# A decoder layer on one core: attention rounds in another order, routing steps with one tensor input, and 110 expert tiles

## The reference

```
x = layernorm(x + mamba(x))                    # state space scan
x = layernorm(x + xattn(x, ctx))               # cross attention, 16 heads of 16 channels, RoPE
x = layernorm(x + ffn(x))                      # mixture of experts and a shared expert

xattn: Q = rope(x)Wq + bq, K = rope(ctx)Wk + bk, V = ctx Wv + bv
       out = softmax(Q K^T / 4) V, then Wo, bo
ffn:   logits = x gate_w^T                     # 15 experts
       the 3 largest are chosen; weights = softmax, renormalised over the 3
       y  = sum over the 3 of weight * ((gelu(x W_g) * (x W_u) * mult) fc2 + b)
       ys = the same with the shared expert's weights, for every token
       out = y + ys
```

## Time and profile before

| | us |
|---|---|
| median of 3 runs | 2185.69 (2179.36 to 2189.15) |
| the profiled execution | 2181.16 |
| its span | 2179.3 |
| busy: PE / DVE / ACT / POOL | 1697.8 / 1588.5 / 1042.0 / 1248.0 |
| granted TensorE clock, mean | 0.906 of full speed |

### The profile page before, as it was taken

How to read it: one execution, slowest core, us unless ns; L and a number is a source line. 1 busy time by engine, 2 the same in 40 slices (tenths; PEclk the granted TensorE clock), 3 DMA queues, 4 the chain that set the end, 5 groups by cost and what they waited for, 6 DMA issues and landing times. The chain is left out here.

```text
span 2179.3 us, 32460 instructions
## 1 busy us (share of the span) xinstructions
PE 1697.8 (78%) x9684; PEld 1089.3 (50%) x9685; DVE 1588.5 (73%) x2792; ACT 1042.0 (48%) x2354; POOL 1248.0 (57%) x840
## 2 busy tenths in 40 slices
PE   5688778778777778534787888777498999999695
PEld 4344444444444444213455555555385555555484
DVE  3699999999899999965478888875223555555278
ACT  3677777777777777620233333333112333333221
POOL 0889888898889899847547776633200222222100
PEclk9899998999899999657799999988699999999897
DMA  5544444555554455414833333331541222222332
GB/s 162 116 115 114 113 111 108 116 117 117 117 117 116 103 123 114 111 60 97 211 106 109 123 105 113 110 106 38 177 163 36 79 82 82 80 81 82 139 128 77
DMA packets 178820, 238.24 MB, mean 109 GB/s; under 512 B 24001, under 2 KB 114113, under 8 KB 176642
## 3 DMA queue, kind: packets, MB, share of 16 engines
q1 hardware_dynamic: 161426, 201.73, 35.4%
q0 software_dynamic: 9984, 28.06, 3.6%
q10 hardware_dynamic: 7280, 6.83, 1.2%
HBM read 169.70 MB, written 66.84 MB: 109 GB/s over the span
## 5 line engine op out<-in xcount | busy, mean ns | idle before, releaser
L268 POOL TENSOR_TENSOR inject<-dx_n,bc_n 128x2048 f32<-128x2048 f32 x128 | 578.9, 4533 | 147.5 <-DMA dx_n<-dup_rows 84.7
L401 ACT ACTIVATE ps_h<-delta_n,a_neg 128x256 f32<-128x256 f32 x1024 | 424.9, 462 | 110.9 <-DVE hc L537 73.5
L524 DVE TENSOR_TENSOR_SCAN ps_h<-ps_h,inject 128x1024 f32<-128x1024 f32 x160 | 365.9, 2287 | 23.8 <-ACT ps_h L401 23.8
L1951 POOL DMA_INDIRECT token_results<-e_y,e_y_row x112 | 106.9, 955 | 389.8 <-DVE e_y L2013 389.5
L1114 ACT ACTIVATE expT<-ps_t 128x512 f32<-128x512 f32 x256 | 147.6, 593 | 307.9 <-PE ps_t L1496 305.7
L1192 DVE TENSOR_REDUCE neg_max<-ps_s 128x2 f32<-128x512 f32 x256 | 172.2, 676 | 123.4 <-PE ps_s L1485 122.9
L524 DVE TENSOR_TENSOR_SCAN h_pool<-ps_h,inject 128x1024 f32<-128x1024 f32 x96 | 218.6, 2278 | 18.9 <-POOL inject L268 14.5
L277 POOL TENSOR_TENSOR h_pool<-h_pool,bc_n 128x1024 f32<-128x1024 f32 x96 | 225.7, 2351 | 0.0
L2041 PE MATMUL e_ps_h<-w,e_xT 128*128 x448 | 219.5, 613 | 7.7 <-issue 6.6
L537 DVE TENSOR_TENSOR hc<-ps_h,bc_n 128x1024 f32<-128x1024 f32 x160 | 195.7, 1223 | 5.9
L1485 PE MATMUL ps_s<-Ks,Qs 96*128 96x256 bf16 x512 | 103.8, 286 | 45.4 <-DVE neg_max L1192 34.9
(11 more groups left out here) (274 smaller groups left out, 3453.0 us busy)
## 6 DMA issues: line engine op xcount, KB each, us to landing
delta_n<-dup_rows SPq DMA_DIRECT2D x128, 256.0 KB, 4.6
dx_n<-dup_rows SPq DMA_DIRECT2D x128, 256.0 KB, 7.6
bc_n<-bc_rows SPq DMA_DIRECT2D x64, 256.0 KB, 4.5
xg<-slot_rows SPq DMA_DIRECT2D x112, 136.0 KB, 2.1
Ks<-k_rows SPq DMA_DIRECT2D x192, 64.0 KB
Qs<-q_rows SPq DMA_DIRECT2D x192, 64.0 KB
e_rows_in<-token_results SPq DMA_DIRECT2D x8, 1536.0 KB, 18.9
dup_rows<-delta SPq DMA_DIRECT2D x32, 256.0 KB, 6.4
```

The costliest lines, as they stand in the source:

```text
L268: nc.gpsimd.tensor_tensor(inject[:, at:at + 2, :, :], dx_n[c // 2][:, None, :, c % 2, :].to_broadcast([P, 2, JB, L]), bc_n[b % 2][:, 0, nq ...
L401: last = nc.scalar.activation(ps_h[k % 2][:, j, :], delta_n[c // 2][:, j, c % 2, :], ACT.Exp, scale=a_neg[:, c, nq, j:j + 1])
L524: nc.vector.tensor_tensor_scan(out.rearrange("p j t -> p (j t)"), ps_h[k % 2][:, :, :].rearrange("p j t -> p (j t)"), inject[:, k % RING, ...
L1951: g.indirect_dma_start(out=y_dram, out_offset=bass.IndirectOffsetOnAxis(ap=y_row[:, j:j + 1], axis=0), in_=y[j][:, 0, :], in_offset=None). ...
```

## The change

Nothing changes in the mamba, table (but for its operands) and combine stages. In the others:

- the heads at which attention's side work stands are others, and `turn_x` and `rope_q` of a sequence move to the end of the round before (there is one more round at the start, which does only these);
- `take_k` goes from DVE to ACT;
- the routing steps are rewritten: `hot` by six `tensor_scalar` (one for each tile and choice, from `iota_e` and a scalar of `choice`) in place of three `tensor_tensor`; `mask` by one `tensor_reduce` and a conversion to bf16 on ACT; the row codes by six `tensor_scalar` and one `tensor_reduce`; PE adds the running rows to the counts in PSUM, so that `slot` falls away, `next_row` is a copy, and `picked` is one `tensor_tensor` with one input in PSUM;
- in the expert stage there are 110 tiles and not 112, POOL makes `e_y_row` by a copy from the code column (unused rows now carry a code of their own, by `fill` and `spare_rows`), SP also waits for that copy (`e_rows`), and DVE does `take_y(t)` ahead of `multiply(t+2)`;
- the spare tiles (14, not 16) are filled by a DMA from DRAM to DRAM.

```
-SLOT_TILES = (T * TOPK // P + NE + 1) // 2 * 2
+SLOT_TILES = T * TOPK // P + NE - 1
-                    sp.wait_ge(zero_made, 1)
-                    sp.dma_start(zero_v[:, NE * REGION:NE * REGION + spare, :],
-                                 ffn.zero[:, :].unsqueeze(1).to_broadcast([P, spare, XW])).then_inc(zeroed, 16)
+                    sp.dma_start(slots_dram[NE * REGION * P:, :], dram["spare_rows"]).then_inc(zeroed, 16)
...
+            def take_mask(b):                                   # ACT, head 8
+                act.wait_ge(route_step, routed(b, MASK))
...
+                nc.scalar.activation(mask[:, :, :], mask_f[:, :, :], ACT.Copy).then_inc(logits_made, 1)
+            def take_k(b):                                      # ACT, head 4; was on DVE, head 4
...
-                for j in range(TOPK):
-                    last = nc.vector.tensor_tensor(hot[:, j, :, :], iota_e[:, :].unsqueeze(1).to_broadcast([P, TT, NE]),
-                                                   choice[:, :, j:j + 1].to_broadcast([P, TT, NE]), ALU.is_equal)
+                for s in range(TT):
+                    for j in range(TOPK):
+                        last = nc.vector.tensor_scalar(hot[:, s, j, :], iota_e[:, :], choice[:, s, j:j + 1], None,
+                                                       ALU.is_equal)
...
+                    for j in range(TOPK):
+                        last = nc.vector.tensor_scalar(coded[:, s, j, :], iota_e[:, :], choice[:, s, j:j + 1],
+                                                       row_code[:, t, j:j + 1], ALU.is_equal, ALU.mult)
...
+                nc.vector.tensor_tensor(picked[:, :, :, :], COUNTS[:, 0:TT, :].unsqueeze(2).to_broadcast([P, TT, TOPK, NE]),
+                                        hot[:, :, :, :], ALU.mult)
+                nc.vector.tensor_copy(table.next_row[:, 1 - b % 2, :], COUNTS[:, TT, :]).then_inc(route_step, 1)
...
-                    if real(b) and h in (6, 9, 13):
-                        weigh(b, h // HG - 1)
+                    if real(b) and h in (7, 10, 13):
+                        weigh(b, (h - 7) // 3)
...
+                nc.tensor.matmul(COUNTS, ident[:, :], table.next_row[:, b % 2:b % 2 + 1, :].to_broadcast([P, TT + 1, NE]),
+                                 start=True, stop=False, skip_group_check=True)
+                pe.wait_ge(logits_made, mask_at(b))
...
+                nc.gpsimd.tensor_copy(y_row[:, at:at + 1], xg[t % R][:, bass.ds(e + D, 1)]).then_inc(e_rows, 1)
...
+                take_y(i, j)
                 if left > 2:
                     multiply(t + 2, j + 2)
-                take_y(i, j)
```

More of the change, by code:

```diff
@@ L868, in attention_phase @@
         tri, tri_bf, ones_bf = sb("tri", [P, P]), sb("tri_bf", [P, P], BF16), sb("ones_bf", [P, P], BF16)
-        iota_e, row_code = sb("iota_e", [P, NE]), sb("row_code", [P, NT])
+        iota_e, row_code = sb("iota_e", [P, NE]), sb("row_code", [P, NT, TOPK])
         choice = sb("choice", [P, TT, TOPK])
-        hot = sb("hot", [P, TOPK, TT, NE])
-        pair, mask = sb("pair", [P, TT, NE]), sb("mask", [P, TT, NE], BF16)
-        slot = sb("slot", [P, TT, NE])
-        picked = sb("picked", [P, TOPK, TT, NE])
+        hot = sb("hot", [P, TT, TOPK, NE])
+        coded = sb("coded", [P, TT, TOPK, NE])
+        mask_f, mask = sb("mask_f", [P, TT, NE]), sb("mask", [P, TT, NE], BF16)
+        picked = sb("picked", [P, TT, TOPK, NE])
         slot_f = sb("slot_f", [P, TOPK, TT])
@@ L1147, in take_logits @@
                                      ACT.Copy).then_inc(logits_made, 1)
+            def take_mask(b):
+                act.wait_ge(route_step, routed(b, MASK))
+                if b >= 1:
+                    act.wait_ge(counted, b)
+                nc.scalar.activation(mask[:, :, :], mask_f[:, :, :], ACT.Copy).then_inc(logits_made, 1)
+            def take_k(b):
+                act.wait_ge(p_k, b + 1)
+                if b >= 1:
+                    act.wait_ge(k_split, b)
+                for c in range(DC):
+                    last = nc.scalar.activation(kb[:, c, :], ps_m[0][:, c, :], ACT.Identity, bias=bk[:, c:c + 1])
+                last.then_inc(kb_made, 1)
             later = [(dst, src, route_in) for dst, src in route_loads]
@@ L1193, in row_max @@
                                         negate=True).then_inc(h_max, 1)
-            def take_k(b):
-                v.wait_ge(p_k, b + 1)
-                if b >= 1:
-                    v.wait_ge(k_split, b)
-                for c in range(DC):
-                    last = nc.vector.tensor_scalar(kb[:, c, :], ps_m[0][:, c, :], bk[:, c:c + 1], None, ALU.add)
-                last.then_inc(kb_made, 1)
             def rope_q(b):
@@ L1323, in make_hot, with make_mask @@
                 last.then_inc(route_step, 1)
-            def add_pair(b):
+            def make_mask(b):
                 v.wait_ge(route_step, routed(b, HOT))
-                nc.vector.tensor_tensor(pair[:, :, :], hot[:, 0, :, :], hot[:, 1, :, :], ALU.add).then_inc(route_step, 1)
-            def make_mask(b):
-                v.wait_ge(route_step, routed(b, PAIR))
-                nc.vector.tensor_tensor(mask[:, :, :], pair[:, :, :], hot[:, 2, :, :], ALU.add).then_inc(route_step, 1)
+                if b >= 1:
+                    v.wait_ge(logits_made, mask_at(b - 1))
+                nc.vector.tensor_reduce(mask_f[:, :, :], hot[:, :, :, :].rearrange("p s j e -> p s e j"), AXX,
+                                        ALU.add).then_inc(route_step, 1)
@@ L1338, in make_code @@
                 last.then_inc(route_step, 1)
             def finish_code(b):
[L1341 to L1346 removed]
                 v.wait_ge(route_step, routed(b, CODED))
[L1348 to L1350 removed]
+                nc.vector.tensor_reduce(X[:, b * TT:(b + 1) * TT, D:D + NE],
+                                        coded[:, :, :, :].rearrange("p s j e -> p s e j"), AXX,
@@ L1351, in take_counts @@
                                         ALU.add).then_inc(route_step, 1)
             def pick_slots(b):
-                v.wait_ge(route_step, routed(b, SLOT))
-                for j in range(TOPK):
-                    last = nc.vector.tensor_tensor(picked[:, j, :, :], slot[:, :, :], hot[:, j, :, :], ALU.mult)
-                last.then_inc(route_step, 1)
+                v.wait_ge(counted, b + 1)
+                nc.vector.tensor_tensor(picked[:, :, :, :], COUNTS[:, 0:TT, :].unsqueeze(2).to_broadcast([P, TT, TOPK, NE]),
+                                        hot[:, :, :, :], ALU.mult)
@@ L1916, in steps @@
                     body(i, j, 2 * R)
[L1917 to L1919 removed]
+            for t in range((ROUNDS - 2) * R, SLOT_TILES):
+                body(t // R, t % R, SLOT_TILES - t)
         def expert(eng, t):
@@ L2286 @@
     }
+    fill = _np.zeros((P, XW), _np.float32)
+    fill[:, D:D + NE] = _np.arange(NE * P, dtype=_np.float32).reshape(NE, P).T
+    spare = _np.zeros((SPARE_TILES * P, XW), _np.float32)
+    spare[:, D + NE - 1] = NE * P + _np.arange(SPARE_TILES * P, dtype=_np.float32)
+    arrays.update(fill=fill, spare_rows=spare)
     arrays = {k: _np.ascontiguousarray(a) for k, a in arrays.items()}
```

265 lines of the change are left out of this document (137 added, 128 removed).

## The result

The changed kernel takes 2116.95 us (median of 4 runs, 2116.38 to 2117.46) against 2182.53 for the kernel before: a ratio of 0.9705 (95% interval 0.9684 to 0.9726). It is faster, as forecast, but lies outside the range of 2122 to 2166. The profiled executions have spans of 2179.3 and 2115.6 us, 64 us apart where 45 were forecast.

| stretch | before | after | difference | forecast |
|---|---|---|---|---|
| to attention's first rotation | 972.6 | 968.2 | -4.4 | 0 |
| from there through round 1 | 124.8 | 124.6 | -0.2 | -1.5 |
| nine rounds, 4 to 12 | 279.5 | 254.4 | -25.1 | -31.1 |
| rounds 2, 3, 13, 14 | 111.8 | 104.7 | -7.2 | -6 |
| round 15 to the end of attention | 68.5 | 67.3 | -1.2 | 0 |

A forecast was written before the change was run, and what follows sets the result against it. Attention's round was taken as a chain alternating between DVE and PE, with no engine full. Rounds -31.1 and -6, start -1.5, experts -6.6 sum to -45: 2136 from the profiled 2181.2, 2140 as median, range 2122 to 2166.

The forecast's parts named there:

- the path through a round: Attention: DVE never waiting from head 0 to 9, then V, then PE alone, last DVE's head 15.
- the part on the experts: Expert stage: two tiles less give -6.6 us; PE nearly full, at most 9 us more possible, taken as 0.
- The waits of the new instructions for POOL: DVE in attention: one wait for each group, `hot` 0.3 us and codes 0.8, likeliest error, bounds 0 and 6.
- rival C: Attention: all twelve `tensor_scalar` and two of `X` wait for POOL, 13.3 us a round, 2255 in all; chance 0.07 with its like.
- The sum of a round: Attention's new chain: 16.7, 3.9, 4.5 and 2.2 us make 27.3, taken as 27.6 with the clock.
- rival B: Attention: no block on new instructions, no chain through the codes, rounds of 26.3 us, experts -8, 2125 in all; chance 0.15.
- The clock: Attention: a round is as long at clock 0.94 as at 1.00; in the new chain PE's 8 us cost 0.4 more.
- what a light DVE alone gives: Attention's round at 1403.94, old order, no e_down products, DVE 23.76 us: 30.5 us as a bound of the period.
- rival A: Attention: the order helps little, chains re-form at other heads, rounds of 29.5 us, about 2161 in all; chance 0.22.
- Start and tail: First rounds: K's copy off DVE gives -1.5 us; spare tiles' DMA 0, bounds -5 and +8; tail 0.
- the signs named beforehand: Rounds 27 to 28 us, `ps_s` waits under 2.5, `picked` about 0.24, reduces near 0.23, POOL's waits some 2, results at 3.28.

The follow-up runs named there:

- exp_old: Changed kernel with DVE's product ahead of the result again and `e_code` and `e_y_row` as two DVE copies: 2127.2 us, ratio 0.9749, 3.218 a tile.
- slice_dve: Changed kernel, old expert order, two small DVE instructions again, `e_y_row` by a maximum with a column picked at run time: 2133.9 us, 0.9788, 3.300 a tile.
- mul_first: Changed kernel with only DVE's old order in the expert tile, product ahead of the result: 2114.6 us, ratio 0.9694, 3.098 a tile.
- order_only: Changed kernel with the routing's old instruction forms and K's biased copy on DVE, so only attention's new heads are left there: 2126.1 us, ratio 0.9752.
- before_y_first: Kernel before with only DVE's expert order changed, the result ahead of the product: 2174.1 us, ratio 0.9960, 3.240 a tile.

## Why the prediction was wrong

The sign and the path through a round were right, and the round nearly so (27.6 forecast, 28.1 at full clock); the size was wrong. One step alone carried it out of the range: with the expert stage at its measured 22.0 us in place of 6.6, the forecast would have been 2124.6, inside.

**The step that failed.** It is in the part on the experts: "Room on PE is 364.3 - 355.4, so at most 9 us more could be won, and I take 0." PE's busy time was read as work that can't shrink. It holds stalls: PE is shown busy for 98% of the stage in both kernels, with tiles of 3.28 and 3.14 us, and where nothing delays it a tile takes 3.02. In the earlier trace rows DVE is busy for only 197 of 364 us, and that was read as room, though its waits inside a turn of the loop ended with the expert's number and with ACT, none with PE. The chain of 3.23 us was there to be added up. The trace has 355.41 busy us for work that then took 336.03 with 2 tiles less: 3.20 and 3.08 busy us a tile for the same matmuls. For judging how close a kernel is to its roofline, the Trainium skill ("Perfetto Trace Analysis", the note at its head) calls matmul busy time a bad metric, because matmuls are pipelined. The trace agrees that it is a bad metric, and here it hid stalls. Taken in this order of edits, the 22.0 us divide as the runs show: 2 x 3.28 = 6.6 for two tiles; 0.064 x 109 = 7 for the run-time column of `lane`, by exp_old against the kernel before (0.082 where slice_dve puts such a column back); 0.12 x 109 = 13 for the two copies in the old order (exp_old less mul_first); and -0.044 x 109 = -5 for the new order. In another order of edits the shares would differ: the same swap is worth +0.04 in the kernel before. The forecast's bound of 9 us beside the two tiles was passed by 6: 15.4 came.

**The waits of the new instructions for POOL** were taken as one for each group, 0.3 and 0.8 us, from the three `picked`. They are 1.2 and 1.5. A small instruction is held until the POOL instruction ends, passes in the gap, and the next but one is held by POOL's next. That is the mechanism of rival C at a fifth of its size, 2.8 us and not 13.3, since only five of the twelve are held, for 0.30 to 0.85 us each (`hot` twice, the codes three times), and `X` is not. The forecast named this as its likeliest error. The rule of the Trainium skill that was weighed there ("SBUF — State Buffer", section Who interferes with whom) agrees with these rows: `tensor_scalar` held, reduces and the product with an input in PSUM free.

**The sum of a round** (27.6, and 28.09 came). Heads 0 to 9 were put at 16.7 us and took 17.4 (1202.45 to the end of `a_res` at 1219.85); V 3.9 and 3.9; PE alone 4.5 and 4.4; head 15 2.2 and 2.2. The path was the one described. The cause given beside it was wrong: DVE was to lose 3.3 us and lost 1.45, and order_only shows that hardly any of the round's gain needed a changed instruction: old forms and K on DVE at the new heads give 28.4. The total came nearest to rival B (2125), but not for its reasons: B had rounds of 26.3 us and 8 us in the experts.

**The clock.** "With PE at a clock of 0.94 its 8 us cost 0.4 more": rounds 9 and 11 took 29.78 and 29.73, 1.7 more. PE is busy for 1.7 us more in them, and all of it shows. The nine rounds fell short by 6.0 us: 9 x 0.49 = 4.4 for the round itself and 3.3 for the clock in these two, less 1.7 for round 12, which is that much shorter. That a round is as long at 0.94 as at 1.00 held for rounds 4 to 9 of the kernel before, and the prediction took it for the others too. It doesn't hold there. before_y_first has the same attention: its round 3 takes 32.01 us at 0.95, where the kernel before has 30.31 at 1.00, and its round 12 came at full clock (columns as in the earlier trace rows):

```profile
1405.32:1434.13 28.81, 23.47 (x193) 16.48 (x192) 23.75 (x67) 11.09 (x26) 16.54 (x27) 1.00 0.36 114
```

The prediction has this round with 30.50 us, at 0.94, as "what a light DVE alone gives". At full clock a light DVE beside a light POOL gives 28.8 without any new order, so the upper bound of 30.5, and what spoke for rival A, was 1.7 us of clock.

**Start and tail.** K's copy on ACT was given 1.5 us of the start. The stretch came out even, since the new heads make the fill up to the first row maximum longer, from 29.6 us to 40.8 in order_only, and K's copy on ACT gives most of it back (31.4 to 32.1). The spare rows' DMA is 0 in round 1 (36.48 and 37.20), as taken.

**What stays open.** The 4.4 us ahead of attention and the 3.0 in the table stage are not shown to be the change's. The first rotation starts between 965.1 and 975.9 in fourteen other profiles, and the experts' first result comes 32.8 to 35.8 us after the last transposed input of the shared expert (36.4 in the profile before) in kernels that don't differ there. The forecast also added 4.5 us, by which the median before lay above the profiled execution; the changed kernel's median lies 0.5 below its own, so that term was spread between runs.

**Of the signs named beforehand**, right or nearly: rounds of 28.1 at full clock (27 to 28 named), `picked` at 0.24, reduces at 0.25. Wrong: DVE's waits on `ps_s` of 3.04 us and not under 2.5, POOL's waits of 2.9 and not 2, results 3.14 apart and not 3.28.
